# Gathering the first 32 rows ahead of the other 96 in a recommender kernel on one core

## The reference

```python
e = stack([tbl_f[ids[:, f]] for f in range(39)], axis=1)      # 1024 x 39 x 16
x0 = xk = e
for W in (f0, f1, f2):                                        # (39*39, 128), (128*39, 128), (128*39, 128)
    z = einsum('bfd,bgd->bfgd', x0, xk).reshape(b, f * g, d)
    xk = einsum('bpd,pm->bmd', z, W); outs.append(xk)
z = concatenate(outs, axis=1).sum(-1)                         # 1024 x 384
h = relu(concatenate([z, dense_ctx], 1) @ W_top1 + b_top1)
y = relu(h @ W_top2 + b_top2) @ W_top3
```

## Time and profile before

| | us |
|---|---|
| median of 3 runs | 1327.42 (1327.40 to 1328.85) |
| the profiled execution | 1329.63 |
| its span in the profile | 1327.8 |
| mean granted TensorE clock | 0.982 of full |
| first chunk on PE starts at | 83.10 |
| first chunk of the second group | 120.84 |

### The profile page before, as it was taken

One profiled execution on the slowest core, in us unless ns is written; L12 is line 12 of the kernel. 1 busy time (PEld: TensorE's weight loads), 2 busy tenths in 40 slices (PEclk: granted clock), 3 DMA queues, 4 the chain that ended last, 5 costly groups with the idle time before them and its releaser, 6 DMA issues. The chain is left out here.

```text
span 1327.8 us, 21824 instructions
## 1 busy us (share of the span) xinstructions
PE 1258.0 (95%) x6649; PEld 974.3 (73%) x6649; DVE 1079.5 (81%) x2290; ACT 1056.4 (80%) x3394; POOL 705.1 (53%) x666
## 2 busy tenths in 40 slices
PE   1379999999999999999999999999999999999998
PEld 0347777777787777777777777877777777777777
DVE  2058989988888888888887888888887988888893
ACT  2047888888888898888888888888988888888894
POOL 7768656555556655555675546566554642333200
PEclk8689999999999999999999999999999999999999
DMA  5032342220222113220221202221132201211000
GB/s 146 6 103 74 106 122 74 64 60 15 73 76 61 46 25 88 63 57 24 54 76 53 61 17 72 76 60 45 32 84 61 57 23 52 79 49 55 11 1 1
DMA packets 61159, 76.43 MB, mean 58 GB/s; under 512 B 16507, under 2 KB 28107, under 8 KB 60998
## 3 DMA queue, kind: packets, MB, share of 16 engines
q1 hardware_dynamic: 44009, 68.76, 17.7%
q0 software_dynamic: 10160, 2.98, 2.2%
q10 hardware_dynamic: 6872, 3.30, 1.0%
HBM read 11.17 MB, written 0.98 MB: 9 GB/s over the span
## 5 line engine op out<-in xcount | busy, mean ns | idle before, releaser
L630 ACT ACTIVATE scaled_x<-Y,x_col 128x128 f32<-128x128 f32 x3072 | 926.4, 508 | 170.1 <-PE Y L956 127.3
L954 PE MATMUL Y<-f_high,cur_high 128*128 128x512 f32 (+1 forms) x1280 | 592.2, 463 | 7.9 <-DVE sum_b L783 6.2
L955 PE MATMUL Y<-f_low,cur_high 128*128 128x512 f32 (+1 forms) x1280 | 499.9, 391 | 0.0
L956 PE MATMUL Y<-f_high,cur_low 128*128 128x512 f32 (+1 forms) x1280 | 499.8, 390 | 0.0
L496 POOL TENSOR_TENSOR pairs<-shifted,base 117x512 f32<-117x512 f32 (+3 forms) x155 | 201.2, 1299 | 396.3 <-PE C L883 343.9
L783 DVE SCALAR_TENSOR_TENSOR sum_a<-Y,x_col,sum_a 128x128 f32<-128x128 f32 x768 | 264.5, 344 | 148.7 <-PE Y L956 145.8
L460 POOL DMA_INDIRECT rows<-in_tbl_dram,ids_sb x312 | 308.2, 988 | 73.3 <-issue 56.8
L954 PEld LDWEIGHTS Y<-f_high,cur_high 128*128 128x128 f32 x1280 | 241.6, 189 | 95.1 <-issue 30.0
L955 PEld LDWEIGHTS Y<-f_low,cur_high 128*128 128x128 f32 x1280 | 242.8, 190 | 81.0 <-issue 44.7
L802 DVE TENSOR_REDUCE cur<-scaled_x 128x128 f32<-128x1920 f32 x128 | 275.6, 2153 | 14.2 <-ACT scaled_x L630 2.4
L956 PEld LDWEIGHTS Y<-f_high,cur_low 128*128 128x128 f32 x1280 | 241.3, 188 | 51.4
(11 more groups left out here) (117 smaller groups left out, 849.3 us busy)
## 6 DMA issues: line engine op xcount, KB each, us to landing
shifted<-x_seq SPq DMA_DIRECT2D x64, 234.0 KB
shifted<-x_seq SPq DMA_DIRECT2D x31, 254.0 KB
shifted<-x_seq SPq DMA_DIRECT2D x31, 252.0 KB
shifted<-x_seq SPq DMA_DIRECT2D x31, 250.0 KB
base<-x_seq SPq DMA_DIRECT2D x95, 78.0 KB
rows<-in_tbl_dram,ids_sb POOLq DMA_INDIRECT x312
base_left<-base_left SPq DMA_DIRECT2D x62, 80.0 KB
left_pairs<-left_pairs SPq DMA_DIRECT2D x62, 80.0 KB
```

The lines of the kernel that those rows point to most:

```text
L630: ins = act.activation(scaled_x[:, :, PLACE[c] + i], where[:, i * M:(i + 1) * M], ACT.Copy, scale=x_col[:, t // JT % QG, t % JT, f:f + 1])
L954: pe.matmul(where, ch, wh, start=True, stop=False)
L955: pe.matmul(where, ch, wl, start=False, stop=False)
L956: pe.matmul(where, cl, wh, start=False, stop=True).then_inc(y_filled, 1)
```

## The change

The first batch tile's ids come in two pieces. POOL gathers 32 rows from each of the 39 tables (34, the mark, 5), and ACT and DVE copy the first 34 fields while the last five arrive. PE turns 32 rows only, into two banks, and two reads (one ACT, one DVE) give the first group's `x_seq`. After the first rows are taken POOL gathers the other 96 rows from each table (39 more DMAs), copies them (`take_rows(0)`), and then gathers 10 fields of the second batch tile. PE turns the 96 rows at slots 28, 30, 32 and 34 of group 0. Group 0 has no sums for group 1 in its slots any more: after its last chunk PE does `scalars(1)`, group 1's seven sums and `scalars(2)`; DVE makes group 1's seven pairs (as it made group 0's, 117 rows each) after its last tile of group 0, then the prepared `f0_left` and the split. All of group 1's copies are SP's. From group 2 on the pairs are POOL's as before; the copies of 127 and 125 rows are each issued as 117 rows and the rest. The second batch tile's other 29 gathers are spread over tiles 4 to 9, its `take_rows` stands at tile 10 and its turns at slots 30, 32, 34 and 36 of group 2. `cur1` has five places instead of six, and the warm-up has 22 products.

```diff
-EARLY = 16
-FIRST_EARLY = 4
-AHEAD = 10
-WARM_FIELDS, WARM_PRODUCTS = 5, 28
+EARLY = 10
+LAST_FIELDS, WARM_PRODUCTS = 5, 22
...
+def at_x(g):
+    bt, q = divmod(g, QG)
+    if g == 0:
+        return 0, (28, 30, 32, 34)
+    if q != 2 or bt + 1 == BT:
+        return None, ()
+    return bt + 1, (30, 32, 34, 36) if bt == 0 else (5, 15, 19, 23)
...
 def gathers_in_tile(t):
-    if t < TPB - AHEAD:
-        n, tiles = NF - EARLY, TPB - AHEAD
-        return 1, range(EARLY + n * t // tiles, EARLY + n * (t + 1) // tiles)
...
+    for bt in range(1, BT):
+        at = TPB * (bt - 1)
+        lo, hi = {1: (4, 10), 2: (11, at + 6)}.get(bt, (at - 8, at + 6))
...
         def _(sp):
-            sp.dma_start(ids_sb[:], ids.rearrange("(t p) f -> p t f", p=P)).then_inc(ids_in, 16)
+            sp.dma_start(ids_first[:], ids[0:GB, :]).then_inc(ids_first_in, 16)
+            sp.dma_start(ids_rest[:], ids[GB:P, :]).then_inc(ids_rest_in, 16)
+            sp.dma_start(ids_sb[:], ids[P:B, :].rearrange("(t p) f -> p t f", p=P)).then_inc(ids_in, 16)
...
-            pool.wait_ge(ids_in, 16)
-            gather(0, range(NF - WARM_FIELDS))
-            pool.memset(warm_mark[:], 0.0).then_inc(warm, 1)
-            gather(0, range(NF - WARM_FIELDS, NF))
-            pool.wait_ge(gathered, 16 * NF)
-            pool.tensor_copy(*row_part(2 * NF, NF)).then_inc(first_rows, 1)
-            pool.wait_ge(first_rows, 4)
-            gather(1, range(FIRST_EARLY))
+            pool.wait_ge(ids_first_in, 16)
+            early = NF - LAST_FIELDS
+            for f in range(early):
+                gather(rows[0:GB, :], ids_first[:], 0, f, first_gathered)
+            pool.memset(warm_mark[:], 0.0).then_inc(warm, 1)
+            for f in range(early, NF):
+                gather(rows[0:GB, :], ids_first[:], 0, f, last_gathered)
+            pool.wait_ge(first_rows, FIRST_STEPS)
+            pool.wait_ge(ids_rest_in, 16)
+            for f in range(NF):
+                gather(rows[0:P - GB, :], ids_rest[:], 0, f, rest_gathered)
+            for j in range(len(ROW_PARTS)):
+                take_rows(0, j)
+            pool.wait_ge(rows_taken, len(ROW_PARTS))
+            pool.wait_ge(ids_in, 16)
+            gather_rows(1, range(EARLY))
...
             for g in range(NG):
                 for j in range(JT):
                     tile(JT * g + j, g, g % QG, j)
+                if g == 0:
+                    make_pairs(1)
...
+                    split_cur0(1)
...
-                    if s in AT_SUM and g + 1 < NG:
+                    if s in AT_SUM and FIRST <= g + 1 < NG:
                         cur0_sum(g + 1, AT_SUM.index(s))
-                    if s == AT_SCALARS and g + 2 < NG:
+                    if s == AT_SCALARS and 0 < g and g + 2 < NG:
                         scalars(g + 2)
                     chunk(t, c)
+                if g == 0:
+                    scalars(1)
+                    for k in range(K0):
+                        cur0_sum(1, k)
+                    scalars(2)
```

More of the change, by code:

```diff
@@ L42 @@
 FIRST_ROWS = [SEL] * KT + [2 * NF]
+SPLIT = (1, 3)
+COPIES = [2 if k in SPLIT else 1 for k in range(KT)]
 LEFT_FIELD, LEFT_PARTNER, LEFT_RUNS = EXTRA, EXTRA + FAR, 4
@@ L48 @@
 RING = 3
+FIRST = 2
 def ring_uses():
-    uses = [(0, k) for k in range(K0)] + [(g, k) for g in range(1, NG) for k in range(KT)]
+    uses = [(g, k) for g in range(NG) for k in range(K0 if g < FIRST else KT)]
     return {u: n for n, u in enumerate(uses)}, [K0 * g + k for g, k in uses]
@@ L530, in _ @@
                     if now and now[0] > 1 and now[1][0] == 0:
[L531 to L532 removed]
+                        pool.wait_ge(rows_taken, len(ROW_PARTS) * now[0])
+                    ks = ((0, 1, 2), (3, 4, 5), ("left", "low"), ())[j] if FIRST <= g + 1 < NG else ()
                     for i in range(max(len(ks), len(fs))):
@@ L541, in _ @@
                         if i < len(fs):
-                            gather(now[0], fs[i:i + 1])
-                    if q == 1 and j >= 2 and bt + 1 < BT:
+                            gather_rows(now[0], fs[i:i + 1])
+                    if bt == 0 and q == 2 and j == 2:
+                        for part in range(len(ROW_PARTS)):
+                            take_rows(1, part)
+                    if bt and q == 1 and j >= 2 and bt + 1 < BT:
                         for part in ((0, 1), (2, 3))[j - 2]:
@@ L733, in _ @@
-            for k in range(K0):
-                r = FIRST_ROWS[k]
-                if k >= RING:
-                    dve.wait_ge(cur0_summed, k - RING + 1)
-                if k == 0:
-                    dve.wait_ge(first_read, 4)
-                    dve.wait_ge(based[0], 16 * BLK)
-                    shift = x_cols(0, 0)[0:r, :]
-                else:
-                    if k >= POOL_COPY:
-                        dve.wait_ge(pool_copied, 16 * POOL_COPIES)
-                    else:
-                        dve.wait_ge(copied[k - 1], 16)
-                    shift = shifted[0:r, k - 1, :] if k < KT else left_pairs[0:r, :]
-                dve.tensor_tensor(pairs[0:r, k % RING, :], shift, base[0:r, 0, :], ALU.mult).then_inc(first_pairs, 1)
+            early = NF - LAST_FIELDS
@@ new lines, in _, with make_pairs @@
+            dve.wait_ge(first_gathered, 16 * early)
+            for lo, n in ((NF, early), (2 * NF, early), (SEL, P - SEL)):
+                dve.tensor_copy(*row_part(lo, n, 0, GB)).then_inc(first_rows, 1)
+            dve.wait_ge(last_gathered, 16 * LAST_FIELDS)
+            for lo in (NF, 2 * NF):
+                dve.tensor_copy(*row_part(lo, NF, early, GB)).then_inc(first_rows, 1)
+            dve.wait_ge(first_filled, 2)
+            dve.tensor_copy(*first_x(1)).then_inc(first_read, 1)
+            def make_pairs(g):
+                for k in range(K0):
+                    r, z = FIRST_ROWS[k], RING_USE[g, k]
+                    if z >= RING:
+                        dve.wait_ge(cur0_summed, READ_BY[z - RING] + 1)
+                    if k == 0:
+                        if g:
+                            dve.wait_ge(x_read, JT)
+                        else:
+                            dve.wait_ge(first_read, 2)
+                        dve.wait_ge(based[g], based_by(g))
+                        shift = x_cols(0, g)[0:r, :]
+                    elif k < KT:
+                        dve.wait_ge(copied[k - 1], copied_by(g, k))
+                        shift = shifted[0:r, k - 1, :]
+                    else:
+                        dve.wait_ge(far_copied, 32 * (g + 1))
+                        shift = left_pairs[0:r, :]
+                    dve.tensor_tensor(pairs[0:r, z % RING, :], shift, base[0:r, g, :], ALU.mult)\
+                       .then_inc(first_pairs, 1)
@@ L749, in split_cur0 @@
+            make_pairs(0)
             def split_cur0(g):
```

266 lines of the change are left out of this document (139 added, 127 removed).

## The result

| | before | changed |
|---|---|---|
| median, us | 1327.93 | 1353.45 (1351.80 to 1355.89, 4 runs) |
| the profiled execution | 1329.63 | 1351.80 |
| its span | 1327.8 | 1350.1 |
| first chunk | 83.10 | 75.24 |
| first chunk of group 1 | 120.84 | 140.66 |

The ratio is 1.0194, with an interval of 1.0181 to 1.0207: slower by 25.5 us, where 9.9 were forecast. It lies outside the range (1315 to 1349). Four more runs, beside three of the experiments, gave 1353.42.

The account below looks back on a forecast made before the run. PE, busy 95% of the span, was taken as the bound. At full gather price the terms gave +19.4 us; cheaper gathers returned 9.5, leaving +9.9 on 1327.4, so 1337.3 us, range 1315 to 1349.

Parts of the forecast that it names:

- Ids, -1.5: Start: the first gather waits for 32 x 39 ids instead of 1024 x 39, between 0 and -2.5 us, taken as -1.5.
- The price of a gather with fewer rows, -9.5: POOL's split gathers: 1.9 ns a row, 1.07 us apart for 32 rows and 1.19 for 96, giving 9.5 us back.
- Rival A: Gathers: price fixed, 78 at 1.20 to 1.25 us, +16.7 to +19.4 us, 1344 to 1347 us; chance 0.33.
- R: Group 0: time when the other 96 rows are ready, 114.3 us at the full gather price.
- 13 us or so: Slot 28 of group 0: PE waits this long for POOL's copies of the other 96 rows.
- From R to group 1's first chunk, 22.5: Gap between groups 0 and 1: DVE's last tiles, pair, seven sums and split end 22.5 us after the rows are ready.
- Group 1, +1: Group 1 starts with empty banks, so PE runs into DVE's pace for a few slots: +1 us (0 to 3).
- Group 2, +2.4: Slot 30 of group 2: PE waits 2.4 us for the copies of rows, with no slack to win it back.
- Rival C: Groups 1 and 2: POOL becomes the bound, PE waits 5 to 10 us in group 2, 1345 to 1352 us; chance 0.06.
- Nothing, for the split copies: Copies of 127 and 125 rows issued in two: no effect, as SP has room and PE hardly waits for pairs later.
- Later groups unchanged: After group 2's wait: groups keep their length; wrong if the groups after the third change theirs.

Follow-up runs that it names:

- the turns behind the group: Changed kernel with the four sets of turns of the other 96 rows moved behind group 0's last chunk: 1341.88 us, ratio 1.0103.
- the second profile: Another profile of the changed kernel with nothing edited: span 1352.0 us.
- the run with more gathers ahead: Changed kernel with 25 instead of 10 of the second batch tile's gathers issued ahead: 1351.92 us, ratio 1.0174.

## Why the prediction was wrong

The mechanism was right in the main, gains at the start against a wait and a gap. The price of a gather, the way from the rows to group 1's first chunk and group 2 were sized too low, and what was forecast of group 1 did not happen. In the order of the steps:

- **Ids, -1.5.** The first gather starts 2.75 us earlier, not 1.5. The 1.2 us more came as a gain.
- **The price of a gather with fewer rows, -9.5.** This step failed first. The 0.34 us by which a gather is longer than a plain copy were taken as half work for each index; they are fixed, and the slope is some 0.8 ns a row, beside 0.55 for the plain copy and the 1.9 chosen. The first 39 gave back 2.7 us (52.99 us from first to last start before, 50.30 now, with a block in both). The second 39 gave back nothing: 1.26 us apart on average, since some stood beside DVE's pairs and took up to 1.41. That is 2.3 of 9.5, and the miss is 7.2 us. Rival A, given 0.33, had this price. The rule that the prediction took from the Trainium skill (DMA: Bandwidth & Descriptors, Anatomy of one DMA), a small cost of descriptors, came out as the trace has it: 920 ns for 96 rows, 867 for 32.
- **R.** The forecast had 104.8 (114.3 less 9.5); measured 109.9. Of the 5.1 us, 7.2 are the price, less 1.2 for the ids and 0.9 for landing and copies. The wait at slot 28 was 13.67 us, "13 us or so" in the forecast, and that is luck: PE came there at 96.4 and not at 92, the first chunk being 3 us later than forecast, and the rows came 5 later.
- **From R to group 1's first chunk, 22.5.** It took 30.8: a miss of 8.3 us, the largest. The chain over DVE's last tile was rightly named as what bounds it, but two links were too short. DVE's third tile ended at R + 6.6, as forecast (6.4); the last one took 13.3 us more and not the 7.9 of a tile without waits, so it ended at R + 19.9, since PE, between turns, fed it chunks too slowly (rounds of 3.2 to 4 us; in a row ahead of the chunks the turns cost as much). The sums took 8.72 us, mostly at the lower clock, not 6.0 at the full one; kept at the full level they took 6.60. The turns' place is worth 8.4 to 9.1 us in this group (the turns behind the group).
- **Group 1, +1.** It became 2.1 us shorter (0.7 in the second profile, which began it at the lower clock), and group 3 1.3 shorter. The forecast had PE run into DVE's pace. It does so in the kernel before, at slot 7, for 1.62 us in group 1 and 1.18 in group 3 (PE's timeline of before):

```profile
127.64 0.50 PE L954 MATMUL Y<-f_high,cur_high 128*128 128x512 f32 x1 [1.62 <-DVE sum_b L783]
```

After the gap, and after the long group 2, DVE is not behind, and both waits are gone. That makes 4.4 us that the forecast had not given back.

- **Group 2, +2.4.** The wait for the copies was that (2.6), but the group took 7.7 more. The turns two chunks apart wait for one another (2.3 us), and PE is at the lower clock for some 3 us behind its wait; in a row they were no better (45.86). With copies earlier and turns four apart 6.6 of it went; what each of the two is worth stays open. Rival C had named group 2, for another reason, which the run with more gathers ahead ruled out.
- **Nothing, for the split copies.** They are split from group 2 on, where the kernel before with and without the split shows the same lengths; no run has the changed kernel without them. Put into the kernel before from group 1 on, they are worth 4.9 us.
- **Later groups unchanged.** They are shorter by 0.07 us on average, 1.8 in all; open.

The misses add up: 7.2 - 1.2 - 0.9 + 8.3 - 4.4 + 5.3 - 1.8 = 12.5, against 22.3 - 9.9 = 12.4 us of span. Rival A's 16.7 to 19.4 us were nearer, since it had the price right, and short of 25.5 by the same gap and group 2.

Open are the 0.07 us of the later groups, the shares of copies and turns in group 2, and the pauses of PE on the one chip, which no run took apart.

## What to carry to other kernels

Before splitting a gather, ask what it costs per instruction: with 0.84 of 0.92 us fixed, a second set of 39 is a second full bill, and the first set hardly gets cheaper. When an operand comes late, put its consumer behind all work that doesn't need it: moving four turns from slot 28 to the end of the group was worth 11.5 us (8.4 to 9.1 of them in that group), because the engines in order behind them could use the wait. And try a change's parts alone. The split copies (4.9 us) and the subtractions moved out of the gathers' way (5.5 us, not a part of this change) make the kernel 0.8% faster, together with two small parts that show no gain clear of noise (ids apart, early copies). The idea that they came with makes it 1.9% slower.

## What was not expected of the hardware

- A DMA of 127 rows of 2 KB held its pair until 96.4 us after an issue near 83, and SP's next issue took 4.28 us; with 117 rows and the rest, issues took 0.79 at most and no pair on POOL waited over 0.6 us for one.
- Three DVE subtractions with both operands in SBUF held one gather for 6.24 us; moved, the longest of the first 39 gathers took 1.32 and the whole kernel 5.5 us less.
- The same DVE cast of 16x128 took 2.05 us in three profiles and 0.22 to 0.25 in the others, but for those from the chip with the pauses; no run shows why.
- A gather costs 867, 920 and 940 ns for 32, 96 and 128 rows of 64 bytes.
- One of the chips ran the kernel before in 1342 instead of 1328 us, with PE waiting up to 3.2 us between plain products around its first turns, and once 40 us.
